# Reordering TensorE's plain and rounded float32 matmuls inside the attention units of a perceiver layer

## What is computed

```python
xn, ln = layernorm(ctx), layernorm(latents)
q = (ln @ Wq)                                  # 16 heads of 64
kv = concatenate([xn @ Wkv, ln @ Wkv])         # 1024 + 64 rows
qn, kn = rmsnorm(q, qn_g) * 64 ** -0.5, rmsnorm(k, kn_g)
attn = softmax(qn @ kn.T)                      # 64 x 1088 per head
out = (attn @ v) @ Wout + bout
```

## Time and profile before

| what | value |
|---|---|
| time, median of 3 runs | 241.36 us (241.01 to 242.09) |
| time of the profiled execution | 241.57 us |
| span of the profiled execution (first to last instruction) | 239.8 us |
| PE busy / its mean granted clock | 95% / 0.983 of full speed |
| DVE, ACT, POOL busy | 64%, 63%, 35% |
| units 1 to 7 of the attention | about 72 to 146 us |
| units 8 to 14 | about 146 to 194 us |

### The profile page before, as it was taken

How to read it: one execution, slowest core, us unless ns; L and a number is a source line. 1 busy time by engine, 2 the same in 40 slices (tenths; PEclk the granted TensorE clock), 3 DMA queues, 4 the chain that set the end, 5 groups by cost and what they waited for, 6 DMA issues and landing times.

```text
span 239.8 us, 4238 instructions
## 1 busy us (share of the span) xinstructions
PE 228.3 (95%) x1493; PEld 197.8 (83%) x1493; DVE 153.5 (64%) x345; ACT 150.1 (63%) x328; POOL 83.3 (35%) x128
## 2 busy tenths in 40 slices
PE   7599999999999999999999999999999998999994
PEld 7365887786888888898888979899999987999883
DVE  1759999997597887767676655666765540312541
ACT  4245579888867668695957477787777755005141
POOL 5458866775746546363431500000000010100200
PEclk9869999999999999999999999999999999999998
DMA  6875100100000000000000699800000000000000
GB/s 175 301 214 206 42 28 25 43 25 22 2 22 0 0 1 4 0 0 3 0 3 0 188 401 351 207 3 0 0 4 0 3 1 0 3 0 0 3 0 22
DMA packets 11237, 13.80 MB, mean 58 GB/s; under 512 B 1585, under 2 KB 9937, under 8 KB 10961
## 3 DMA queue, kind: packets, MB, share of 16 engines
q1 hardware_dynamic: 10944, 13.01, 16.9%
q10 hardware_dynamic: 272, 0.52, 0.7%
HBM read 13.14 MB, written 0.13 MB: 55 GB/s over the span
## 4 chain that ended last, share of the span: by engine, by line
PE 70%; DVE 13%; issue 4%; ACT 4%; DMA 3%; POOL 2%; SPq 1%; ACTq 0%; DVEq 0%; POOLq 0%
PE banks L1121 17%; PE banks L1002 13%; PE banks L1047 9%; PE banks L1076 8%; PE banks L1142 5%; PE banks L1239 5%; DVE small L773 4%; DMA rows<-in_L_xattn_ln_x_b 3%; PE banks L1135 3%; DVE sk L785 3%; PE banks L1078 2%; PE banks L1169 2%; DVE raw L741 2%; PE banks L1264 1%; DVE small L747 1%
## 5 line engine op out<-in xcount | busy, mean ns | idle before, releaser
L808 DVE TENSOR_TENSOR ptl<-banks,pth 128x512 fp32r<-128x512 f32 (+1 forms) x48 | 26.8, 558 | 27.3 <-ACT pth L574 26.4
L1121 PE MATMUL banks<-xnh,pth 128*128 128x256 f32 x128 | 37.5, 293 | 0.0
L1121 PE MATMUL banks<-xnh,ptl 128*128 128x256 f32 x128 | 36.2, 283 | 0.0
L1121 PE MATMUL banks<-xnl,pth 128*128 128x256 f32 x128 | 36.2, 283 | 0.0
L458 POOL TENSOR_TENSOR small<-small 128x16 f32<-128x16 f32 x8 | 23.3, 2908 | 33.3 <-DVE small L780 33.3
L574 ACT ACTIVATE pth<-banks 128x512 fp32r<-128x512 f32 (+1 forms) x48 | 23.7, 493 | 11.8 <-PE banks L1002 10.6
L521 ACT ACTIVATE sk<-banks 128x512 f32<-128x512 f32 x36 | 20.6, 606 | 15.8 <-PE banks L1047 15.7
L785 DVE TENSOR_TENSOR sk<-banks,small 128x512 f32<-128x512 f32 x36 | 23.0, 679 | 7.6 <-POOL small L458 7.6
L773 DVE TENSOR_REDUCE small<-sk 128x8 f32<-128x512 f32 x36 | 23.5, 678 | 4.9 <-ACT sk L521 4.8
L1002 PE MATMUL banks<-ident,sp 128*128 128x128 f32 x144 | 24.4, 279 | 0.7 <-ACT sp L555 0.5
L1121 PEld LDWEIGHTS banks<-xnh,pth 128*128 128x128 f32 x128 | 24.5, 191 | 0.4 <-issue 0.4
(11 more groups left out here) (175 smaller groups left out, 486.0 us busy)
## 6 DMA issues: line engine op xcount, KB each, us to landing
knT<-in_L_attn_qkv_kernel SPq DMA_DIRECT2D x1, 3072.0 KB, 13.3
raw<-in_ctx SPq DMA_DIRECT2D x16, 128.0 KB, 2.0
knT<-in_L_xattn_Wq SPq DMA_DIRECT2D x1, 1024.0 KB, 9.1
wv<-in_L_xattn_Wkv SPq DMA_DIRECT2D x1, 1024.0 KB, 5.2
wout_sb<-in_L_xattn_Wout SPq DMA_DIRECT2D x1, 1024.0 KB, 5.7
knT<-in_L_attn_out_kernel SPq DMA_DIRECT2D x1, 1024.0 KB, 16.0
wraw<-in_L_xattn_Wkv ACTq DMA_DIRECT2D x1, 512.0 KB, 4.0
wraw<-in_L_xattn_Wkv SPq DMA_DIRECT2D x1, 512.0 KB, 6.4
```

The source lines that it names most:

```text
L808: nc.vector.tensor_tensor(ptl[:, j0:j1, :], banks[:, t3_bank(u, c), 0:(j1 - j0) * P].rearrange("p (j r) -> p j r", j=j1 - j0), pth[:, j0:j ...
L1121: nc.tensor.matmul(banks[:, u_bank(u), 0:D], p_[:, j, :], x_, start=(j == 0 and i == 0), stop=False)
```

## The change

- **Units 8 to 14 (`unit_alone`).** The calls on PE are put in the order probs_transposed 0 and 1, mix_transposed(u - 1), probs_transposed 2, values(u - 1), attended, logits part 2, then logits parts 0 and 1, mix. So all plain matmuls of a unit stand ahead of all its rounded ones.
- **Units 0 to 7 (`unit_of_keys`).** In units 1 to 7, probs_transposed 2 and logits part 2 follow values(u - 1) directly, ahead of project; in unit 0 only logits part 2 moves ahead of parts 0 and 1.
- **Banks.** The last third of the transposes goes to bank 2 (the keys' bank) in units 1 to 7, with a wait for the copy of the keys' first half, and into columns of the mix's own bank in units 8 to 14, with a wait for `heads_out(u - 2)`; `mix(u)` of units 8 to 14 now waits until `ptl` holds all three thirds before it starts. The second third of unit 7 goes to bank 1.
- **ACT and DVE.** `probs_high(u, 2)` comes right after `probs_high(u, 1)` (before heads_out and squares), `probs_low(u, 2)` ahead of `key_norm2`; ACT's copy to `uT` comes ahead of the copy of the feed-forward weights.
- **Semaphores.** Logits part 1 instead of part 2 now signals that a unit's logits are complete; part 2 waits for the maximum of the unit before.

```diff
--- before.py
+++ after.py
@@ -328,7 +328,13 @@
 
         def t3_bank(u, c):
 
-            return 6 if c != 1 or 0 < u < G else (7 if u == 0 else 0)
+            if u == 0:
+                return 7 if c == 1 else 6
+            if u < G:
+                return 2 if c == 2 else (1 if c == 1 and u == G - 1 else 6)
+            if c == 2 and u < UNITS - 1:
+                return u_bank(u)
+            return 0 if c == 1 else 6
 
         def u_bank(u):
 
@@ -647,12 +653,12 @@
                 if u > 0:
                     mix_out(u - 1)
                 probs_high(u, 0)
+                if u > 0:
+                    mixT_out(u - 1)
                 if w1T_first < u <= w1T_first + len(w1T_blocks):
                     r = u - w1T_first - 1
                     act.wait_ge(w1T_ps, r + 1)
                     nc.scalar.activation(w1T_blocks[r][1], banks[:, 5, D:2 * D], ACT.Copy).then_inc(w1T_ready, 1)
-                if u > 0:
-                    mixT_out(u - 1)
                 if i < ITEMS:
                     keys_out(i, 0)
                     keys_out(i, 1)
@@ -661,6 +667,8 @@
                 if u == 0:
                     unit_high(1)
                 probs_high(u, 1)
+                if 0 < u < UNITS - 1:
+                    probs_high(u, 2)
                 if u > 0:
                     heads_out(u - 1)
                 if i + 1 < ITEMS:
@@ -668,7 +676,8 @@
                     squares(i + 1, 1)
                 if u in (2, 3):
                     mask_bias(1, u == 3)
-                probs_high(u, 2)
+                if u in (0, UNITS - 1):
+                    probs_high(u, 2)
                 if i + 1 < B * NT:
                     context_high(i + 1)
                 if split_unit(u + 2):
@@ -892,11 +901,14 @@
                 probs_low(u, 1)
                 if u > 0 and i + 1 < ITEMS:
                     unit_low(u + 1)
+                if u > 0:
+                    probs_low(u, 2)
                 if i + 1 < ITEMS:
                     key_norm2(i + 1, 0)
                     key_norm2(i + 1, 1)
                     key_clamp(i + 1)
-                probs_low(u, 2)
+                if u == 0:
+                    probs_low(u, 2)
                 if u + 1 < UNITS:
                     logits_max(u + 1)
                 if i + 1 >= ITEMS and split_unit(u + 2):
@@ -1062,9 +1074,10 @@
 
                     pe.wait_ge(kt_ready, 2 * ITEMS_A - (1 if part == 1 else 2))
                     pe.wait_ge(kn_ready, 2 * ITEMS_A)
+                elif part == 2:
+                    pe.wait_ge(max_ready, u)
                 elif part == 0:
                     pe.wait_ge(kt_ready, 2 * ITEMS_A if b == 0 else 2 * ITEMS)
-                    pe.wait_ge(max_ready, u)
                 c0, c1 = ((0, 512), (512, 1024), (1024, KW))[part]
                 dst = banks[:, 3 + part, 0:c1 - c0]
                 if split_unit(u) and part < 2:
@@ -1073,10 +1086,10 @@
                     for i, (q_, k_) in enumerate(((qh, k_high), (ql, k_high), (qh, k_low))):
                         if i == 1 and part == 0:
                             pe.wait_ge(kl_ready, splits(u))
-                        nc.tensor.matmul(dst, q_[:, u % 2, :], k_, start=(i == 0), stop=(i == 2))
-                    return
-                ins = nc.tensor.matmul(dst, qbd[:, u, :], knT[:, b, g, c0:c1], start=True, stop=True)
-                if part == 2:
+                        ins = nc.tensor.matmul(dst, q_[:, u % 2, :], k_, start=(i == 0), stop=(i == 2))
+                else:
+                    ins = nc.tensor.matmul(dst, qbd[:, u, :], knT[:, b, g, c0:c1], start=True, stop=True)
+                if part == 1:
                     ins.then_inc(s_ps, 1)
 
             def probs_transposed(u, c):
@@ -1085,12 +1098,13 @@
                     pe.wait_ge(exp_ready, u + 1)
                 if c == 2:
                     pe.wait_ge(twice_ready, u + 1)
-                if u == 0 or u > G:
-
-                    if 3 * u + c - (1 if c == 2 else 2 if c == 1 else 0) > 0 and not (u == 0 and c == 1):
-                        pe.wait_ge(ptl_ready, 3 * u + c - (1 if c == 2 else 2 if c == 1 else 0))
-                elif u < G or c != 1:
-                    pe.wait_ge(ptl_ready, 3 * u + c - (1 if u == G and c == 2 else 0))
+                if t3_bank(u, c) == 6 and c > 0:
+
+                    pe.wait_ge(ptl_ready, 3 * u + 1)
+                if 0 < u < G and c == 2:
+                    pe.wait_ge(kt_ready, 2 * (ITEMS_A + u) + 1)
+                if G <= u < UNITS - 1 and c == 2:
+                    pe.wait_ge(o_ready, u - 1)
                 transposes(banks[:, t3_bank(u, c), :], lambda i: block_of(u, j0 + i), j1 - j0).then_inc(pt_ps, 1)
 
             def mix(u, parts=(0, 1, 2)):
@@ -1100,8 +1114,11 @@
                     pe.wait_ge(lns_ready, 1)
                 if u == 0:
                     pe.wait_ge(ptl_ready, 2)
+                elif u == UNITS - 1:
+                    pe.wait_ge(o_ready, u - 1)
                 elif u >= G:
-                    pe.wait_ge(o_ready, u - 1)
+
+                    pe.wait_ge(ptl_ready, 3 * u + 3)
                 else:
                     pe.wait_ge(o_ready, u)
                 for c in parts:
@@ -1158,7 +1175,7 @@
                     project(i, 1)
             keys_transposed(ITEMS_A - 1, 0)
             keys_transposed(ITEMS_A - 1, 1)
-            for part in range(3):
+            for part in (2, 0, 1):
                 logits(0, part)
             keep_clock(12, 7)
             def attended(g):
@@ -1168,42 +1185,56 @@
                     pe.wait_ge(w_tail["wout"], 16)
                 return nc.tensor.matmul(banks[:, 2, 0:D], oT[:, g, :], wout_sb[:, g, :], start=(g == 0), stop=(g == G - 1))
 
-            for u in range(UNITS - 1):
+            def unit_of_keys(u):
+
                 i = ITEMS_A + u
                 probs_transposed(u, 0)
-                if u >= G:
-                    logits(u + 1, 0)
                 if u > 0:
                     mix_transposed(u - 1)
-                if i < ITEMS:
-                    keys_transposed(i, 0)
-                    keys_transposed(i, 1)
+                keys_transposed(i, 0)
+                keys_transposed(i, 1)
                 if i + 1 < ITEMS:
                     norm_transposed(tile(i + 1))
                 probs_transposed(u, 1)
-                if u >= G:
-                    logits(u + 1, 1)
                 if u > 0:
                     values(u - 1)
+                    probs_transposed(u, 2)
+                    logits(u + 1, 2)
                 if i + 1 < ITEMS:
                     project(i + 1, 0)
                     project(i + 1, 1)
-                if u < G:
-                    logits(u + 1, 0)
-                    logits(u + 1, 1)
+                if u == 0:
+                    logits(u + 1, 2)
+                logits(u + 1, 0)
+                logits(u + 1, 1)
+                if u == 0:
+                    probs_transposed(u, 2)
+                mix(u)
+
+            def unit_alone(u):
+                for c in range(2):
+                    probs_transposed(u, c)
+                mix_transposed(u - 1)
                 probs_transposed(u, 2)
+                values(u - 1)
+                if u > G + 1:
+                    attended(u - G - 2)
                 if w1T_first < u <= w1T_first + len(w1T_blocks):
                     pe.wait_ge(w1T_ready, u - w1T_first)
-                logits(u + 1, 2)
+                for part in (2, 0, 1):
+                    logits(u + 1, part)
                 mix(u)
-                if u > G + 1:
-                    attended(u - G - 2)
                 if w1T_first <= u < w1T_first + len(w1T_blocks):
 
                     r = u - w1T_first
                     pe.wait_ge(w_tail["ffn_a"], 32)
                     pe.wait_ge(max_ready, u + 2)
                     transposes(banks[:, 5, D:2 * D], lambda j: w1T_blocks[r][0][:, j, :], 2).then_inc(w1T_ps, 1)
+
+            for u in range(G):
+                unit_of_keys(u)
+            for u in range(G, UNITS - 1):
+                unit_alone(u)
 
             u = UNITS - 1
             probs_transposed(u, 0)
```

## The result

The changed kernel takes 244.61 us (median of 4 runs, 244.45 to 245.25), the kernel before 241.37: ratio 1.014, 95% interval 1.0124 to 1.0156. It is slower by 3.2 us. The forecast was 244.4, in a range of 242.4 to 245.9. The profiled execution took 244.53 us with a span of 242.7, for which 242.8 was forecast.

A forecast was written before the change was run, and what follows sets the result against it. PE, busy 95% of the span, was taken as the bound. Terms -0.2 + 4.4 - 0.85 - 0.35 = +3.0 on 241.57 profiled give 244.6; the median lies 0.2 lower, 244.4 us, range 242.4 to 245.9.

The forecast's parts named there:

- The new wait: Units 8 to 14: PE stands still before values until ACT's copy to `uT` is there, 0.63 per unit, +4.4 us.
- Switches of kind: Grouping plain and rounded matmuls saves 0.03 per unit, -0.2 us in all; upper bound 1.7 by lengths.
- the rival: Switching kinds is dear: by lengths 1.7 saved in place of 0.2, giving 242.9 us; chance 0.07.
- The earlier maximum: Units 8 to 10 and 15: the maximum starts earlier, so transposes no longer wait for the exponentials, -0.85 us.
- Mix waiting for all of `ptl`: Units 8 to 14: mix's wait for all of `ptl` is covered by values, attended and logits, 0.7 to spare; cost nothing.
- Units 1 to 7: Last third and part 2 fill PE's 0.16 hole ahead of project; -0.35 us, bounds 0 and -1.0.
- the keys' chain: Project, squares, norm, power, key_scale, keys_transposed: slack 0.16, then it binds with a period of 10.83 against 10.79.
- in unit 6, no chain takes the 0.33 back: Behind the last project, in unit 6, the 0.33 of PE work moved ahead of project stays gained.
- the wait of the second third on `ptl`: Units with keys: the second third waits for `ptl` behind key_scale on DVE, 0.73 after the keys are there.
- losses of 0.04 in five periods: Units with keys: 0.04 lost in each of five periods, cancelling with late exponentials of unit 3 won, to within 0.05.
- Sum: Whole kernel: the terms add to +3.0 us on the profiled execution of 241.57, giving 244.6.
- The clock: Rival: clock falls over eleven transposes and a gap, 1.9 us without a true matmul; 9.8 more, 254 us; chance 0.02.

The follow-up runs named there:

- experiment 1: Changed kernel, units 8 to 14: last third of the transposes moved ahead of mix_transposed, so nothing lies between the mix's transposes and values; 245.31 us, ratio 1.0156.
- experiment 3: Changed kernel, units 8 to 14: attended and logits part 2 ahead of values(u-1), ACT's weights' copy ahead of the first third; 240.89 us, ratio 0.9972.
- experiment 4: Changed kernel, units 8 to 14: values(u-1) between logits parts 0 and 1, behind attended and part 2; ACT copies weights ahead of uT; 240.44 us, ratio 0.9956.
- Experiment 2: Changed kernel, units 8 to 14: plain logits part 2 put between rounded parts 0 and 1, one more switch per unit; 244.40 us, ratio 1.0123.
- Experiment 7: Kernel before, units 8 to 14: on ACT alone, the last third is rounded ahead of heads_out; 240.27 us, ratio 0.9957.
- experiment 8: Changed kernel with POOL's power for the keys' norm replaced by a product in units 0 to 7; 243.21 us.
- experiment 9: Kernel before with POOL's power for the keys' norm replaced by a product; 241.34 us, ratio 1.0005.

## Why the prediction was right

**The new wait.** Forecast 0.63 per unit and 4.4 in all. The trace gives 0.64 by the starts of unit 12, experiment 1 moves it by 0.11 per unit when one transpose less covers it, and when PE gets other work there, experiment 3 takes away 0.63 in each of units 10 to 14 and experiment 4 about 0.60. Periods forecast at about 7.0 and 7.6 are 6.99, 7.01 and 7.66. Shown.

**Switches of kind.** Forecast 0.2 saved in all, with 1.7 as the bound by lengths. Experiment 2 gives under 0.01 per switch; adding up starts was right, and the rival is out. Even the 0.03 per unit was too much: units 11 to 14 grew by 0.63 with a gap of 0.64, which leaves 0.01 for it.

**The earlier maximum.** Forecast 0.85 given back, and no wait for the exponentials is left in units 8 to 14 of the changed kernel. Experiment 7 gets 0.61 of it with ACT's order alone, in units 9 and 10, where 0.72 was forecast for those two. In the changed kernel the term is only seen as a difference: seven gaps of 0.64 less the 3.53 of units 8 to 15 leave 0.95 for it and for the switches together, against 1.05 forecast.

**Mix waiting for all of `ptl`.** Costed at nothing; the changed kernel's mix follows the logits without a pause, and units 11 to 14 take their old 7.03 plus the gap.

**Units 1 to 7.** Forecast -0.35, the periods give -0.41, but not where the forecast had it, so the nearness is luck. It was right that the keys' chain takes the gain back in the steady units: units 2, 4, 5 and 6 are as long as before, and experiment 8 shows the chain. The step that failed is "in unit 6, no chain takes the 0.33 back". Unit 7 has keys to transpose as well, and it waits for them. Its transposes of `sk`, before and after:

```profile
138.53 1.04 PE L1002 MATMUL banks<-ident,sk 128*128 128x128 f32 x8
```

```profile
138.05 1.25 PE L1014 MATMUL banks<-ident,sk 128*128 128x128 f32 x8
```

Unit 7 is only 0.09 shorter than before, and without the power it loses another 0.23 (8.15 to 7.92). The rest of the -0.41 is 0.13 in unit 1, not traced, and 0.18 in unit 3, which the forecast had set against losses of 0.04 in five periods that did not come. Also wrong was the cause given for the wait of the second third on `ptl`, key_scale: in the kernel before the wait stays when the keys come earlier (experiment 9), and in unit 4 of the changed kernel there is none (transposes of `xn` at 106.78, the second third at 107.00). The period was forecast at 10.83 and is 10.80; the missing wait may be the difference.

**Sum.** Forecast +3.0 for the profiled execution, measured 244.53 - 241.57 = +2.96. The main term and the mechanism were right; that the total comes within 0.04 is luck. The smaller errors cancel in it: +3.53 and -0.41 and an earlier start of 0.18, against +3.35 and -0.35 and none, and the start differs by up to 0.9 between the profiles of this study (last section).

**The clock.** The granted clock stayed at 1.00, the 2.4 GHz level, in each of units 8 to 14, with its eleven transposes in a row (thirteen in units 10 to 14) and its gap, and the logits behind them kept 0.23. Units 8 to 14 of no run here show the fall that the Trainium skill's sentence on transposes ("TensorE: Matmul & The Clock Gate", Part 4: PE-mode transpose) would let one fear.

## What to carry to other kernels

Before matmuls are sorted by kind, price a switch by the distances of starts over a whole group, not by the length of the first one: here a first matmul looked 0.08 dearer and cost under 0.01. What separates a producer from its consumer in a list worked off in order is cover for the trip through the other engine; a sort takes it away, and the price is that trip (0.85 here, from the last transpose to where values really run) less what still lies between. Other work that does not need the copy gives the time back in that place, of whichever kind it is (experiments 3 and 4). And where a hole is filled ahead of a loop that runs through other engines, look at the slack of the loop first: the hole here was 0.16 wide and the slack 0.16, and in the steady units all of the gain went back into a wait.

## What was not expected of the hardware

The printed wait was only 0.36 of a loss of 0.64: matmuls that drain (0.27) hide the beginning of the standstill, and the first matmul after it is 0.11 longer in addition. And the start of the kernel scatters more than the units do: the last mix matmul of unit 0 lies between 71.71 and 72.61 us in the eleven profiles that keep the keys' power, which ahead of it differ only in the order of a few calls, while from unit 15's last mix matmul to the end it is 39.09 to 39.11 us in every one.
